# Full attention of a two-layer tower: queries and keys projected in three chunks of 128 rows instead of four of 96

## The reference

```
h = take(embed, x)                                  # (4, 1024, 192)
h = h + conv_gate_block(layernorm(h))
h = h + routed_attention_and_ffn(layernorm(h))      # 154 selected queries per sequence
h = h + attention(layernorm(h))                     # all 1024 queries, 12 heads of 16
h = h + ternary_ffn(layernorm(h))

# attention:
q, k, v = split(x @ w_attn + b_attn)                # 192 columns each
a  = softmax(q @ k.T) @ v                           # per head
a1 = softmax(q @ mk.T) @ mv                         # 100 memory slots, the same q
alpha = sigmoid(concat(a, a1) @ w_alpha + b_alpha)
out = (alpha * a + (1 - alpha) * a1) @ w_proj + b_proj
```

## Time and profile before

| | us |
|---|---|
| median of 3 runs | 1895.57 |
| lowest, highest | 1887.01, 1904.90 |
| the profiled execution, its own time | 1903.3 |
| its span in the trace | 1901.6 |
| PE busy in the span | 1640.8 (86%) |
| DVE busy | 1287.5 (68%) |
| ACT busy | 998.3 (53%) |
| TensorE clock granted, mean | 0.892 of full |

### The profile page before, as it was taken

The page is one execution under the profiler, slowest core; times in us unless marked ns, Lnnn a source line. Parts: engine busy times, 40 slices in busy tenths (PEclk is TensorE's granted clock), DMA queues, the critical chain, the costliest instruction groups (busy, mean ns, idle before and its releaser), DMA issues.

```text
span 1901.6 us, 26442 instructions
## 1 busy us (share of the span) xinstructions
PE 1640.8 (86%) x9799; PEld 921.1 (48%) x9799; DVE 1287.5 (68%) x3010; ACT 998.3 (53%) x1417; POOL 124.9 (7%) x159
## 2 busy tenths in 40 slices
PE   4789878998999999995476987889899999999935
PEld 2458556663333333363244674756524333333814
DVE  7738643046889999836967577421489899996478
ACT  2432542134777777753542335331457777777345
POOL 6010000000000000004301000000000000000020
PEclk9878896998999999996687698789989999999957
DMA  6021300015001000000000322000430010000001
GB/s 156 0 69 57 82 26 1 1 58 174 26 26 34 26 26 26 9 1 24 27 17 1 117 49 68 1 1 1 133 108 26 27 34 26 26 26 1 1 1 34
DMA packets 53861, 73.39 MB, mean 39 GB/s; under 512 B 18647, under 2 KB 27172, under 8 KB 53734
## 3 DMA queue, kind: packets, MB, share of 16 engines
q1 hardware_dynamic: 52198, 68.55, 12.6%
q0 software_dynamic: 1536, 3.15, 0.7%
HBM read 38.51 MB, written 33.17 MB: 38 GB/s over the span
## 4 chain that ended last, share of the span: by engine, by line
PE 69%; DVE 19%; ACT 5%; issue 3%; DMA 2%; POOL 1%; SPq 1%; DVEq 0%; ACTq 0%; POOLq 0%
PE PV L909 10%; PE ST L893 9%; PE S L859 7%; PE ST L805 4%; PE ST L560 3%; PE MT L859 3%; PE ST L590 3%; DVE nmp L1585 2%; PE PV L918 2%; PE S L816 2%; DVE st L1458 2%; DVE amax L1693 2%; DVE R L1692 2%; PE S L854 1%; DVE Er L1513 1%
## 5 line engine op out<-in xcount | busy, mean ns | idle before, releaser
L1257 ACT ACTIVATE Er<-ST 128x1024 f32<-128x1024 f32 x384 | 377.1, 1021 | 105.9 <-PE ST L893 105.6
L1637 DVE TENSOR_REDUCE nmp<-S 128x1 f32<-128x512 f32 x514 | 337.6, 683 | 30.6 <-PE S L859 30.6
L893 PE MATMUL ST<-QS,KS 100*128 100x512 bf16 x768 | 218.0, 385 | 0.3
L909 PE MATMUL PV<-Er,V 128*17 128x512 f32 x1536 | 211.9, 601 | 0.0
L859 PE MATMUL S<-KS,QS 96*128 96x512 bf16 x514 | 183.3, 392 | 2.2 <-DMA QS<-scr_q 1.4
L1637 DVE TENSOR_REDUCE nmp<-MT 128x1 f32<-128x512 f32 x254 | 173.5, 683 | 13.5 <-PE MT L859 13.5
L859 PEld LDWEIGHTS S<-KS,QS 96*128 96x128 bf16 x514 | 48.2, 98 | 156.3 <-DVE nmp L1637 103.3
L448 POOL TENSOR_SCALAR tp<-mv 128x8 f32<-128x8 f32 x20 | 5.5, 275 | 1660.5 <-DVE mv L1462 1660.5
L1585 DVE TENSOR_REDUCE nmp<-S 128x1 f32<-128x512 f32 x120 | 77.6, 684 | 46.3 <-PE S L675 45.9
L893 PEld LDWEIGHTS ST<-QS,KS 100*128 100x128 bf16 x768 | 72.2, 99 | 64.3 <-ACT Er L1257 5.7
L859 PE MATMUL MT<-KS,QS 96*128 96x512 bf16 x254 | 99.4, 391 | 0.9 <-DVE nmp L1637 0.9
(11 more groups left out here) (398 smaller groups left out, 3133.2 us busy)
## 6 DMA issues: line engine op xcount, KB each, us to landing
KS<-scr_k SPq DMA_DIRECT2D x72, 192.0 KB, 2.6
scr_k<-R SPq DMA_DIRECT2D x16, 576.0 KB, 4.0
QS<-scr_q SPq DMA_DIRECT2D x48, 192.0 KB, 2.8
scr_k<-R SPq DMA_DIRECT2D x16, 384.0 KB, 4.6
QS<-scr_k SPq DMA_DIRECT2D x24, 192.0 KB, 2.7
scr_q<-R SPq DMA_DIRECT2D x8, 576.0 KB, 4.5
scr_k<-R SPq DMA_DIRECT2D x16, 192.0 KB, 5.2
scr_q<-R SPq DMA_DIRECT2D x8, 384.0 KB, 4.8
```

Of the source, the lines that this page charges most:

```text
L893: ins = nc.tensor.matmul(ST[i % 2][:, (kt % 2) * HALF:(kt % 2 + 1) * HALF], KS[0:KP + 4, k, kt * P:(kt + 1) * P], QS[0:KP + 4, k, half * H ...
L909: ins = nc.tensor.matmul(PV[row:row + VC, :], slots[h // H].V[:, kt, h % H, :], E[:, step % RING, (kt % 2) * HALF:(kt % 2 + 1) * HALF], st ...
L1257: A_(E[:, g, :], ST[i % 2][:, :], ACT.Exp).then_inc(s["exps"], 1)
L1637: v.tensor_reduce(nmp[:, u // 2, u % 2:u % 2 + 1], bank, AX.X, ALU.max).then_inc(s["reduced"], 1)
```

## The change

Queries and keys of the full attention are handled in three chunks of 128 rows for each slot. The weight columns of queries and keys lie side by side (queries 0 to 191, keys 192 to 383), so columns 128 to 255 are one chunk, `both`: its first 64 rows are queries 128 to 191, its last 64 are keys 0 to 63. Columns 0 to 127 are the second (`qc`), 256 to 383 the third (`kc`, keys 64 to 191, in the buffer of `both`). The first half now holds `both` and `qc` (four pieces for each slot, as before); the second half holds only `kc` (two pieces for each slot, before four). `FIRST_AT` spreads the 18 units as 4, 4, 4 and 6. `both` is written by two triples of DMAs with 64 rows each, the other chunks by one triple with 128 rows. Heads 0 to 3 take their keys from `both`, heads 0 to 7 their queries from `qc`. Two semaphores are renamed and counts follow (`p * 14` becomes `p * 12`).

```
-FIRST_AT = [FIRST_UNITS[2 * i:2 * i + 2] for i in range(7)] + [FIRST_UNITS[14:]]
+FIRST_AT = [FIRST_UNITS[4 * i:4 * i + 4] for i in range(3)] + [FIRST_UNITS[12:]]
...
-            o.kc = R[0:CH, 0:3 * HALF].bitcast(BF16).rearrange("p (a n) -> p a n", a=3)
-            o.qc = R[0:CH, 3 * HALF:6 * HALF].bitcast(BF16).rearrange("p (a n) -> p a n", a=3)
+            o.both = R[:, 0:3 * HALF].bitcast(BF16).rearrange("p (a n) -> p a n", a=3)
+            o.qc = R[:, 3 * HALF:6 * HALF].bitcast(BF16).rearrange("p (a n) -> p a n", a=3)
+            o.kc = o.both
...
-                for c in range(2):
-                    for o in slots:
-                        write(p, o, o.scr_k, c, o.kc[:, :, :], 8 + 4 * c, ("kw0", "kw1")[c])
-                        write(p, o, o.scr_q, c, o.qc[:, :, :], 10 + 4 * c, ("qw0", "qw1")[c])
-                    if c == 0:
-                        heads1(p, a, range(KRING))
+                for o in slots:
+                    write(p, o, o.scr_k, 0, o.both[D - P:P, :, :], 8, "bothw")
+                    write(p, o, o.scr_q, P, o.both[0:D - P, :, :], 8, "bothw")
+                    write(p, o, o.scr_q, 0, o.qc[:, :, :], 10, "qw")
+                heads1(p, a, range(KRING))
+                for o in slots:
+                    write(p, o, o.scr_k, D - P, o.kc[:, :, :], 12, "kw")
                 heads1(p, a, range(KRING, H))
...
-            def keys_queries(p, o, c):
...
+            def project_rows(p, o, group, off, after=None):
+
+                for j in range(2):
+                    i = group + j
+                    pe.wait_ge(o.s["resid"], p * 12 + i - 1)
+                    for c in range(2):
+                        r = CH + c
+                        ins = nc.tensor.matmul(o.R2[i % 2], wat[0:r, c, off:off + P], o.XT[0:r, c, j * HALF:(j + 1) * HALF], start=c == 0, stop=c == 1)
+                    ins.then_inc(o.s["proj"], 1)
+                    if after is not None:
+                        after(j)
+
+            def both_queries(p, o):
+                evacuated(p, o, 3)
+                project_rows(p, o, 6, P)
+                project_rows(p, o, 8, 0)
+
+            def last_keys(p, o):
+
+                def between(j):
+                    for what in FIRST_AT[2 * o.x + j]:
                         unit(p, what)
...
+                project_rows(p, o, 10, 2 * P, between)
...
-                    act.wait_ge(o.s["kw0"], p * 96 + 96)
-                    act.wait_ge(o.s["qw0"], p * 48 + 48)
-                    cut(p, o, 10, pieces_1(o), HALF)
+                    act.wait_ge(o.s["bothw"], p * 96 + 96)
+                    cut(p, o, 10, pieces_keys(o), HALF)
```

More of the change, by code:

```diff
@@ L153, in build @@
         R1 = acc_out[0:CH, :, :]
+        R1F = acc_out[:, :, :]
         junkg = acc_out[:, :, :].rearrange("p a n -> p (a n)")[:, 0:F]
@@ L280, in pieces_q0, with pieces_both, pieces_keys @@
             return [o.spl0[:, :, m, :] for m in range(2)]
-        def pieces_1(o):
-            return [dst[:, :, j * HALF:(j + 1) * HALF] for dst in (o.kc, o.qc) for j in range(NH)]
+        def pieces_both(o):
+            return [dst[:, :, j * HALF:(j + 1) * HALF] for dst in (o.both, o.qc) for j in range(NH)]
+        def pieces_keys(o):
+            return [o.kc[:, :, j * HALF:(j + 1) * HALF] for j in range(NH)]
         KR = ("kr0", "kr1", "kr2", "kr3")
@@ L349, in load_head, with write @@
                 sp.dma_start(dst[0:KP, h % KRING, :], scr[h * DH:(h + 1) * DH, :, :].rearrange("p j n -> (p j) n")).then_inc(s[done], 16)
-            def write(p, o, scr, c, src, lo, done):
-                sp.wait_ge(o.s["lo"], p * 14 + lo)
-                spread_parts(scr[c * CH:(c + 1) * CH, :, :], src, scr is o.scr_q, o.s[done])
+            def write(p, o, scr, row, src, lo, done):
+                sp.wait_ge(o.s["lo"], p * 12 + lo)
+                spread_parts(scr[row:row + src.shape[0], :, :], src, scr is o.scr_q, o.s[done])
             def keys0(p, o, heads):
@@ L367, in heads1 @@
                     m = o.x * H + h
-                    c = h // 6
-                    sp.wait_ge(o.s[("kw0", "kw1")[c]], p * 96 + 96)
+                    if h < 4:
+                        sp.wait_ge(o.s["bothw"], p * 96 + 96)
+                    else:
+                        sp.wait_ge(o.s["kw"], p * 48 + 48)
                     if m < KRING:
@@ L374, in heads1 @@
                     load_head(KS, o.scr_k, h, KR[h % KRING])
-                    sp.wait_ge(o.s[("qw0", "qw1")[c]], p * 48 + 48)
+                    if h < 8:
+                        sp.wait_ge(o.s["qw"], p * 48 + 48)
+                    else:
+                        sp.wait_ge(o.s["bothw"], p * 96 + 96)
                     load_head(QS, o.scr_q, h, QR[h % KRING])
@@ L380, in _ @@
                     write(p, o, o.scr_k0, 0, o.spl[:, :, 0, :], 2, "kw0")
-                    write(p, o, o.scr_k0, 1, o.spl[:, :, 1, :], 4, "kw1")
+                    write(p, o, o.scr_k0, CH, o.spl[:, :, 1, :], 4, "kw1")
                     if o is a:
@@ L818, in back @@
                     ins.then_inc(o.s["ffn"], 1)
-            def keys_queries(p, o, c):
-                def between(i):
-                    for what in FIRST_AT[4 * o.x + i - 10]:
+            def project_rows(p, o, group, off, after=None):
+                for j in range(2):
+                    i = group + j
+                    pe.wait_ge(o.s["resid"], p * 12 + i - 1)
+                    for c in range(2):
[11 more added lines that the diff above has]
+                    for what in FIRST_AT[2 * o.x + j]:
                         unit(p, what)
[L825 to L828, removed]
+                project_rows(p, o, 10, 2 * P, between)
             def bank_free(p, what):
@@ L1147, in cut @@
             def cut(p, o, group, pieces, width):
+                rows = pieces[0].shape[0]
                 def mid(i):
-                    act.wait_ge(o.s["resid"], p * 14 + i + 1)
-                    A_(pieces[i - group][:, 1, :], R1[:, i % 2, 0:width], ACT.Copy).then_inc(o.s["mid"], 1)
+                    act.wait_ge(o.s["resid"], p * 12 + i + 1)
+                    A_(pieces[i - group][:, 1, :], R1F[0:rows, i % 2, 0:width], ACT.Copy).then_inc(o.s["mid"], 1)
                 for i in range(group, group + len(pieces)):
-                    act.wait_ge(o.s["proj"], p * 14 + i + 1)
-                    A_(pieces[i - group][:, 0, :], o.R2[i % 2][0:CH, 0:width], ACT.Copy).then_inc(o.s["hi"], 1)
+                    act.wait_ge(o.s["proj"], p * 12 + i + 1)
+                    A_(pieces[i - group][:, 0, :], o.R2[i % 2][0:rows, 0:width], ACT.Copy).then_inc(o.s["hi"], 1)
                     if i > group:
@@ L1779, in _ @@
                 for o in slots:
-                    cut(p, o, 6, pieces_1(o), HALF)
+                    cut(p, o, 6, pieces_both(o), HALF)
                 for o in slots:
                     def between(i, p=p, x=o.x):
-                        for what in FIRST_AT[4 * x + i - 10]:
+                        for what in FIRST_AT[2 * x + i - 10]:
                             unit(p, what)
-                    cut(p, o, 10, pieces_1(o), HALF, between)
+                    cut(p, o, 10, pieces_keys(o), HALF, between)
                 attention(p)
```

36 lines of the change are left out of this document (18 added, 18 removed).

## The result

The changed kernel is slower by 0.8%: 1912.98 us (median of 20 runs, 1898.04 to 1923.96) beside 1897.31 us (median of 20 runs of the kernel before, 1886.30 to 1905.51), a ratio of 1.0078 with a 95% interval of 1.0057 to 1.0100, or +14.8 us. (The ratio is not the quotient of the two medians, which lie 15.7 us apart; this text goes by the ratios and their intervals.) The prediction had said 1903, within 1888 to 1917, and "within 1%". Sign and size class hold; its +7.2 us was about half of what came, and two of its steps stand on other ground than it gave.

The account below looks back on a forecast made before the run. Bound by the transfers that set the first unit's start and by the stretch to the row maxima. Each pass +5.5 - 4.0 + 2.1 = +3.6 us, twice +7.2, from 1895.6 to 1902.8 us; range 1888 to 1917.

Parts of the forecast that it names:

- X: Start of the first unit in a pass, set by transfers; predicted to go from 438.2 to 443.7 us.
- the stretch: From first unit to end of the row maxima in each pass; 21.5 us before, DVE nearly full.
- before 441: Sign that the forecast is wrong: the first unit starting earlier than 441 us in the trace.
- Computing at zero cost: First half's eight pieces: 128 rows in place of 96 take PE, ACT and DVE no longer; zero.
- The first half, writing, +5.5 us: Writes ahead of the first load: 1.57 MB more at 284 GB/s, unhidden, +5.5 us a pass.
- rows, not bytes: Rival, chance 0.2: 64, 96 and 128-row writes cost the same; +8.3 on the wait, 1908.4 us in all.
- The stretch at full clock, -4.0 us: First unit to row maxima: eight DVE instructions fewer, 2.25 us of new waits; 17.5 us, was 21.5.
- The clock, +2.1 us: PE's longer wait before the first unit brings half clock over first units and next piece; +2.1 us a pass.
- The upper bound of 5.5: High price of the clock: half clock over the whole stretch, three pieces, 5.5 us a pass; as rival, chance 0.1.
- a stretch over 22 us: Sign that the forecast is wrong: first unit to row maxima lasting more than 22 us.
- The gain without the delay: Rival, chance 0.13: first unit not delayed, or least delay with clock held; at best -4.0 a pass, 1887.6 us.
- Slower for certain: Rival, chance 0.07: 64-row triples write at half rate, 142 GB/s; each pass loses 14.7 us, 1925 us.

Follow-up runs that it names:

- e4: Changed kernel with seven unused f32 matmuls added behind slot `a`'s first piece of the second half, keeping PE busy through the wait; ratio 1.0022 to the kernel before.
- e1: Changed kernel with the loads of slot `a`'s heads 0 to 3 issued ahead of slot `z`'s writes; ratio 0.9984 to the kernel before.
- after_again: The changed kernel run once more without any edit, giving its second trace; ratio 1.0102 to the kernel before.
- e5: Changed kernel with slot `a`'s first loads ahead of slot `z`'s writes and units spread 3, 3, 3, 9; median 1886.99 us, ratio 0.9948.
- e2: Kernel before, with only the loads of slot `a`'s heads 0 to 3 moved ahead of slot `z`'s writes; ratio 0.9982.

## Why the prediction was right, and where not

*What bounds it.* Right. X is set by the transfers that SP's queue issues ahead of the first load, and X and the stretch together carry most of the change. Aligned to its own first piece, the first unit came at 444.1 (410.28 + 33.85), where 443.7 was said. Read by itself, the time of that unit (436.87) would have met the sign "before 441"; that is the shift of the whole pass, and a sign that goes by an absolute time has no defence against it.

*Computing at zero cost.* Right: 128-row operations of 512 columns last as long on DVE as 96-row ones, 0.68 to 0.69 us.

*The first half, writing, +5.5 us.* The size holds (+5.9 and +5.3; +6.3 and +5.8 in the second trace), the step does not. "Bytes over time is what the rows show" is wrong: rows in the fuller half over time is what holds. Two errors nearly cancelled, so the size was luck. At the rates of the writes alone the 3.15 MB in 64-row triples run at 209 GB/s (15.0 us and not the 11.1 that 284 gives), the 3.15 MB in 128-row triples at 396 (8.0 and not 11.1). The sum is 23.0 us against 4.72 MB / 0.295 = 16.0 before, +7.0 for the writes alone. The kernel shows a little less: the queue from first write to first load grew by 6.3, and the load behind it came in 0.4 us sooner.

*The rival "rows, not bytes".* Its mechanism is the true one, and its total, 1908.4 (+12.8), is nearer to the measured +14.8 than the forecast's +7.2. I had held against it that 305 GB/s over 96 rows and 336 over 128 lie too close. The second figure was the error: it scales a stretch with a share of 0.61 up to a full one, and real 128-row writes move 396. Its price of 8.3 was too high, in part because it took 4.15 us for a triple; 3.8 to 4.0 are measured, which gives 7.0, and the kernel shows 5.8.

*The stretch at full clock, -4.0 us.* Nearly right. Computed 17.5, measured 18.2 with PE kept busy (e4), so -3.35: the waits for the fourth unit came to 2.64 us in place of 2.25, which is 0.4 of the 0.7 us between them.

*The clock, +2.1 us.* This is the term that was mis-sized. Against e4's stretch it measured +3.2, +2.1, +5.9 and +3.9 in the four passes of the two traces, 3.8 on average. One pass met the forecast; for the others the step that failed is the one that let half clock end after one piece "as the stretch is dense". With four units between pieces PE is not dense. In the first trace the clock fell a second time behind such a unit, in the second it stayed down through two and three pieces, and e1 shows it falling without a wait for a transfer. The upper bound of 5.5 was exceeded once, by 0.4.

*The sum.* With measured terms: 5.8 - 3.35 + 3.8 = 6.3 us for each pass, twice 12.5. By the ratio the time rose by 14.8. The missing 2 us, and what more after_again has by its time, lie outside of the two distances, in parts that vary by more than that between executions; where they come from stays open. The second execution also meets one of the prediction's signs of being wrong, a stretch over 22 us (24.1 and 22.1).

*The other rivals.* "The gain without the delay" didn't come: the 64-row writes hide nowhere. With both costs taken away (e5) it is real: -10.2 us, of which the order of the loads gives 1.6 (e2), so 8.6 beside its -8. "Slower for certain" had half rate for 64 rows right, but took it as half of 284; the measured 209 is about half of the 128-row rate, and above the 185 from which that rival decides. The expected rival to e1, ACT waiting for the buffer of `z` behind the loads, was not seen.

## What to carry to other kernels

Price a write from SBUF to memory by the rows that it takes in the fuller half of the partitions, not by its bytes (measured with 32 and 64 rows in a half, 12 KiB a row): 64 rows in one half cost what 128 across both do, and a chunk that must be cut is best cut so that its larger part crosses the middle. When work is taken out of a stretch, look at what the rest does to PE: a longer wait ahead of it brought half clock each time, a unit that waits for its bank inside it in some passes and not in others, and the wait and the clock together ate more than the saved work. Before such a change is given up, test its costs one by one; here the saving was real, and the loads issued first with three units between pieces turned 0.8% lost into 0.5% gained.

## What the runs showed of the hardware

- Writes from SBUF to memory: 209 and 210 GB/s for rows 0 to 63 and 64 to 127, 295 for 96 rows, 396 for 128, and 402 for the 64 rows from 32 to 95. Through all of it the DMA share stands at 0.95 to 1.03, so a full share says nothing of the rate.
- Alternating lower and upper halves on one queue gives 228 GB/s, hardly more than one half alone.
- The granted clock fell to its lower level (0.58 on average over 4 us) with no idle time of PE over 1.96 us, behind 4 us in which PE was busy for 2.04 (e1). Behind 4 us with 2.03 busy and an idle time of 1.97 it stayed at 1.00 (e4).
- After a gap of 6.22 us half clock lasted 7 us in one execution and, after one of 6.63 us, 19 us in another of the same program, in which PE was busy without a break for the first 6.6 us.
- Seven f32 matmuls of 512 columns in the wait kept the clock at 1.00 until late in the stretch: 1.0022 in place of 1.0078, and 7.6 us (0.40%) by the stretches.
